# A mixer's layout split into two halves of the partitions, with its core in 64x64 tiles of TensorE

## The reference, cut to what matters

```python
# mixer: per channel d a linear recurrence with 64 states, B and C elementwise
def mixer(x, ...):                       # x is already layernorm(x) of the layer
    xn = layernorm(x) * ln_gamma + ln_beta
    dA = exp(-exp(log_A) * dt[:, None]); dB = B_param * dt[:, None]
    def step(h, u):
        h = dA * h + dB * u[..., None]
        y = einsum('dn,bdn->bd', C_param, h) + D_param * u
        return h, y
    ys = scan(step, 0, xn over time)
    return x + ys @ W_out.T + b_out
x = x + mixer(layernorm(x))
x = x + cross_attention(ctx, ctx, layernorm(x))
x = x + feed_forward(layernorm(x))       # w1, w2, h1, h2, w3
```

## Time and profile before

| | us |
|---|---|
| median of 3 runs | 1049.09 (1048.56 to 1052.2) |
| the profiled execution | 1048.15, its span 1046.4 |
| TensorE busy, whole span | 916.5 (88%) |
| VectorE, ScalarE, GpSimd busy | 576.4, 532.0, 206.2 |
| from 254.3 us on (feed-forward of all blocks, attention of 1 to 7) | 792.1, TensorE busy 773.1 |

### The profile page before, as it was taken

How to read it: one execution, slowest core, us unless ns; L and a number is a source line. 1 busy time by engine, 2 the same in 40 slices (tenths; PEclk the granted TensorE clock), 3 DMA queues, 4 the chain that set the end, 5 groups by cost and what they waited for, 6 DMA issues and landing times.

```text
span 1046.4 us, 15287 instructions
## 1 busy us (share of the span) xinstructions
PE 916.5 (88%) x5059; PEld 726.4 (69%) x5059; DVE 576.4 (55%) x948; ACT 532.0 (51%) x784; POOL 206.2 (20%) x239
## 2 busy tenths in 40 slices
PE   3200998976999999999999999999999999999996
PEld 0000988854778777877787778777877877787885
DVE  6598886663555555545454654555455555453421
ACT  2356675231665366446635663575366536645431
POOL 2365364100400130022003100400040014002000
PEclk9999999995999999999999999999999999999999
DMA  8984332134000200010001001100100020001000
GB/s 256 340 324 142 106 110 77 61 120 187 1 1 1 86 0 0 20 65 0 0 35 50 0 0 45 40 0 0 53 32 0 0 85 0 0 20 41 1 1 22
DMA packets 13502, 60.70 MB, mean 58 GB/s; under 512 B 2579, under 2 KB 4246, under 8 KB 12598
## 3 DMA queue, kind: packets, MB, share of 16 engines
q1 hardware_dynamic: 13382, 60.32, 16.8%
q10 hardware_dynamic: 64, 0.07, 0.0%
q0 software_dynamic: 32, 0.00, 0.0%
HBM read 46.09 MB, written 23.72 MB: 67 GB/s over the span
## 4 chain that ended last, share of the span: by engine, by line
PE 71%; DVE 12%; issue 9%; ACT 4%; DMA 2%; POOL 1%; DVEq 1%; POOLq 0%; ACTq 0%; SPq 0%
PE pair L1050 43%; PE pair L1037 9%; PE pair L1009 3%; PE pair L998 3%; PE pair L469 2%; PE pair L1025 2%; PE pair L461 2%; PE pair L509 2%; PE pair L975 1%; PE pair L1018 1%; DMA V<-V 1%; DVE V L348 1%; DMA ring<-kernel_rows 1%; DVE vbuf L898 1%; DVE V L347 1%
## 5 line engine op out<-in xcount | busy, mean ns | idle before, releaser
L751 ACT ACTIVATE vbuf<-pair,scl 128x512 f32<-128x512 f32 x128 | 87.8, 686 | 237.2 <-PE pair L1050 231.4
L1050 PE MATMUL pair<-h1hi,h_turned 128*128 128x512 f32 x512 | 204.1, 399 | 1.5 <-DVE h1lo L869 1.5
L1050 PE MATMUL pair<-h2hi,h_turned 128*128 128x512 f32 x512 | 202.6, 396 | 0.0
L1050 PE MATMUL pair<-h1lo,h_turned 128*128 128x512 f32 x512 | 199.8, 390 | 0.0
L1050 PE MATMUL pair<-h2lo,h_turned 128*128 128x512 f32 x512 | 199.6, 390 | 0.0
L869 DVE TENSOR_TENSOR h1lo<-vbuf,h1hi 128x512 fp32r<-128x512 f32 x80 | 57.7, 721 | 119.5 <-ACT h1hi L752 118.7
L1050 PEld LDWEIGHTS pair<-h1hi,h_turned 128*128 128x128 f32 x512 | 96.1, 188 | 34.5 <-issue 10.5
L1050 PEld LDWEIGHTS pair<-h2hi,h_turned 128*128 128x128 f32 x512 | 96.1, 188 | 25.2 <-issue 5.9
L869 DVE TENSOR_TENSOR h2lo<-vbuf,h2hi 128x512 fp32r<-128x512 f32 x64 | 44.2, 690 | 123.5 <-ACT h2hi L752 123.5
L1037 PE MATMUL pair<-zThi,w_turned 128*128 128x512 f32 x256 | 105.6, 413 | 5.3 <-DVE vbuf L898 2.7
L1050 PEld LDWEIGHTS pair<-h2lo,h_turned 128*128 128x128 f32 x512 | 96.2, 188 | 19.3
(11 more groups left out here) (117 smaller groups left out, 1484.0 us busy)
## 6 DMA issues: line engine op xcount, KB each, us to landing
h_turned<-d_h SPq DMA_DIRECT2D x2, 4096.0 KB, 14.3
xres<-in_x SPq DMA_DIRECT2D x8, 512.0 KB, 7.0
ring<-alpha_rows SPq DMA_DIRECT2D x16, 256.0 KB, 3.7
ring<-kernel_rows SPq DMA_DIRECT2D x16, 256.0 KB, 3.5
x_rows<-x1t SPq DMA_DIRECT2D x8, 512.0 KB, 2.6
xr<-x_rows SPq DMA_DIRECT2D x8, 512.0 KB, 3.5
out<-xr SPq DMA_DIRECT2D x8, 512.0 KB, 2.6
x_rows<-xres SPq DMA_DIRECT2D x7, 512.0 KB, 2.6
```

Of the source, the lines that this page charges most:

```text
L751: e.activation(vb[:, s % 2, :], h_ps[s % 4], ACT.Gelu, scale=sc)
L1050: ins = e.matmul(bank, w[:, k, m * P:(m + 1) * P], src[part][:, k, :], start=(k == 0 and part == 0), stop=(k == HC - 1 and part == 1))
```

## The change

The host hands over a second copy of x, `xs`, with channels 0 to 127 on partitions 0 to 63 and 128 to 255 on 64 to 127, the partition within a half being the step in a chunk. `tok` [128, 64 chunks, 128] holds it, is normed in place and takes y in the end. `GG` has the kernel entries, `EE` all state matrices (loaded at once in the front; `xres` lies on the same memory and is loaded group by group later), `TT` two buffers of Toeplitz matrices for 16 channels of each half. The statistics of a token lie in two halves of the partitions and are put together in small steps (`chain_step`) for 16 chunks at a time. The core has 16 iterations (`NOCT`) of 8 channels in each half, written out without loops, and three products for a channel, each on 64 rows and 64 columns; the carried product of an iteration runs in the next one, two channels late (`LAG`). The residual base is made in the core and after it. Waits of attention and projection are split between `k_in` (xW, keys, scl) and `w_in`. GpSimd and SP work as in the excerpts. The doublings and the steps of the tail are as they were, `y_turn` reads `tok[:, 8 * i + c, :]`.

```diff
+    def tt_load(e, g):
+        for h in range(2):
+            e.dma_start(TT[g % 2][L * h:L * h + L, :],
+                        bass.AP(t["kr_h"], (8 * h + g) * (GRP * L), [[1, L], [1, GRP * L]])).then_inc(T_in[g % 2], 16)
...
+        e.wait_ge(al_st, 32)
+        for g in range(NGRP):
+            for h in range(2):
+                e.dma_start(EE[L * h:L * h + L, GRP * g:GRP * g + GRP, :].rearrange("p d n -> p (d n)"),
+                            bass.AP(t["alS_h"], (8 * h + g) * (GRP * N), [[0, L], [1, GRP * N]])).then_inc(E_in[g], 16)
+        e.dma_start(bo[:, :], a["ab"].partition_broadcast(P)).then_inc(wo_in, 16)
...
+            tt_load(e, g)
+        for n in ("w1", "w2", "w3", "h1"):
+            e.dma_start(t["d" + n], a[n]).then_inc(w_d, 16)
+        for n in ("xW", "keys", "scl"):
+            e.dma_start(t[n], a[n]).then_inc(k_in, 16)
+        for g in range(NBLK):
+            e.wait_ge(h_ps, 2 * g + 2)
+            e.dma_start(xres[:, 4 * g:4 * g + 4, :], a["x"][:, 4 * g:4 * g + 4, :]).then_inc(xr_in[g], 16)
+            if g == 4:
+                e.wait_ge(w_d, 64)
+                for n in ("w1", "w2"):
+                    e.dma_start(t[n].bitcast(F32), t["d" + n]).then_inc(w_in, 16)
+        for n in ("h1", "w3"):
+            e.dma_start(t[n].bitcast(F32), t["d" + n]).then_inc(w_in, 16)
+        e.dma_start(t["dh2"], a["h2"]).then_inc(w_d, 16)
...
+        def inverse(b):
+            e.wait_ge(chain, 10 * b + 10)
+            here = slice(SB * b, SB * b + SB)
+            e.tensor_tensor(rs[:, :, here], sv[:, :, here], mhalf[:, :, :], ALU.pow).then_inc(powd, 1)
 
         def gamma(g):
+            e.wait_ge(z_rdy, 8 * g + 8)
+            v = tok[:, 8 * g:8 * g + 8, :]
+            e.tensor_tensor(v, v, gam[:, :].unsqueeze(1).to_broadcast([P, 8, P]), ALU.mult).then_inc(z_g, 1)
+        inverse(0)
+        e.wait_ge(bc_in, 64)
+        inverse(1)
+        gamma(0)
+        gamma(1)
+        inverse(2)
+        gamma(2)
+        gamma(3)
+        inverse(3)
+        gamma(4)
+        gamma(5)
+        for h in range(2):
+            rows = slice(L * h, L * h + L)
+            e.wait_ge(shift, 4)
+            e.wait_ge(z_g, 6)
+            e.tensor_scalar_add(rsn[rows, :], rs[rows, 0, h:BC:2], 1.0).then_inc(natural, 1)
+            e.wait_ge(natural, 2 * h + 1)
+            e.tensor_scalar_add(ngn[rows, :], ng[rows, 0, h:BC:2], 0.0).then_inc(natural, 1)
+
+        def mask(g):
+            e.wait_ge(T_in[g % 2], 32 * (g // 2 + 1))
+            e.wait_ge(natural, 4)
+            e.wait_ge(base_b, 4 * max(g - 4, 0))
+            for h in range(2):
+                e.wait_ge(t_mask, 2 * g + h)
+                v = TT[g % 2][L * h:L * h + L, :].rearrange("p (d t) -> p d t", d=GRP)
+                e.affine_select(out=v, in_=v, compare_op=ALU.is_ge, fill=0.0, base=L - 1,
+                                pattern=[[0, GRP], [-1, L]], channel_multiplier=-1).then_inc(t_mask, 1)
+
+        def bias(tile):
+            if tile == 0:
+                e.wait_ge(wo_in, 32)
+            e.wait_ge(base, tile + 1)
+            e.wait_ge(t_mask, min(2 * (tile // 4 + 5), 2 * NGRP))
+            e.tensor_tensor(xres[:, tile, :], xres[:, tile, :], bo[:, :], ALU.add).then_inc(base_b, 1)
+        for g in range(4):
+            mask(g)
+        for g in range(4, NGRP):
+            mask(g)
...
+        def row_evac(v):
+            for h in range(2):
+                u = 2 * v + h
+                e.wait_ge(k_ps, v + 1)
+                if u >= 4:
+                    e.wait_ge(kr_st[u % 4], 16)
+                e.activation(ksb[:, u % 4, :], kps[v % 2][h], ACT.Copy).then_inc(k_ev, 1)
+            for h in range(2):
+                u = 2 * v + h
+                e.wait_ge(k_ev, u + 1)
+                c = (1 - h) * (P * L) + v * 2048
+                e.dma_start(kr[0, c:c + 2048].rearrange("(q m) -> q m", q=4), ksb[0:P:32, u % 4, :]).then_inc(kr_st[u % 4], 16)
+
+        def norm_apply(b):
+            e.wait_ge(shift, b + 1)
+            for c in range(SB * b, SB * b + SB):
+                e.activation(tok[:, c, :], tok[:, c, :], ACT.Identity, bias=ng[:, 1, c:c + 1], scale=rs[:, 1, c:c + 1]).then_inc(z_rdy, 1)
+
...
+        def entry_exp(g):
+            e.wait_ge(E_in[g], 32)
+            v = EE[:, GRP * g:GRP * g + GRP, :].rearrange("p d n -> p (d n)")
+            e.activation(v, v, ACT.Exp, scale=esc[:, :]).then_inc(e_rdy, 1)
 
         def residual_base(g):
+            e.wait_ge(xr_in[g], 16)
+            for j in range(4 * g, 4 * g + 4):
+                e.activation(xres[:, j, :], xres[:, j, :], ACT.Identity, bias=ngn[:, j:j + 1], scale=rsn[:, j:j + 1]).then_inc(base, 1)
+        for v in range(4):
+            row_evac(v)
+        e.wait_ge(const, 9)
+        norm_apply(0)
+        entry_exp(0)
+        norm_apply(1)
+        entry_exp(1)
+        entry_exp(2)
+        norm_apply(2)
+        entry_exp(3)
+        norm_apply(3)
+        for g in range(4, NGRP):
+            entry_exp(g)
+        e.wait_ge(natural, 4)
+        for o in range(NOCT):
+            e.wait_ge(y_ps, o + 1)
+            e.activation(tok[:, :, OCT * o:OCT * o + OCT], yps[o % 4].rearrange("p (i c) -> p c i", i=OCT), ACT.Copy).then_inc(y_out, 1)
+            if o % 2 == 1 and o // 2 + 2 < NGRP:
+                tt_load(e, o // 2 + 2)
+            if o % 2 == 1 and o >= 5:
+                residual_base((o - 5) // 2)
+        residual_base(NBLK - 2)
+        residual_base(NBLK - 1)
 
...
+        def stats(b, steps):
+            for c in range(SB):
+                if c % 8 == 0:
+                    e.wait_ge(x_in[2 * b + c // 8], 16)
+                e.bn_stats(st4[:, b % 2, c, 0:2, :].rearrange("p a m -> p (a m)"), tok[:, SB * b + c, :]).then_inc(stat, 1)
+                if steps and c >= 4:
+                    steps.pop(0)()
+
+        def beta(g):
+            e.wait_ge(*((z_g, g + 1) if g < 6 else (z_h, g - 5)))
+            v = tok[:, 8 * g:8 * g + 8, :]
+            e.tensor_tensor(v, v, bet[:, :].unsqueeze(1).to_broadcast([P, 8, P]), ALU.add).then_inc(z_b, 1)
+        stats(0, [])
+        stats(1, [lambda n=n: chain_step(0, n) for n in range(11)])
+        stats(2, [lambda n=n: chain_step(1, n) for n in range(11)])
+        e.wait_ge(bc_in, 64)
+        beta(0)
+        beta(1)
+        stats(3, [lambda n=n: chain_step(2, n) for n in range(11)])
+        e.wait_ge(k_ps, 4)
+        for row in (0, N):
+            e.tensor_copy(GG[row:row + 1, :, L - 1], edit[row:row + 1, 1, :]).then_inc(g_row, 1)
+        for n in range(10):
+            chain_step(3, n)
+        beta(2)
+        beta(3)
+        chain_step(3, 10)
+        for k in range(2):
+            e.memset(dec[:, k, :].rearrange("p (b c) -> p b c", c=CH)[:, :, 0], 0.0).then_inc(dec0, 1)
+        beta(4)
+        beta(5)
...
+        def state(o, c):
+            i = OCT * o + c
+            for h in range(2):
+                rhs = tok5[L * h:L * h + L, i, :, 0:CH - 1]
+                rows = slice(N * (1 - h), N * (2 - h))
+                out = hps[o % 2][rows, c * BC:(c + 1) * BC].rearrange("p (b c) -> p b c", b=BATCH)[:, :, 1:CH]
+                ins = e.matmul(out, EE[L * h:L * h + L, i, :], rhs, start=True, stop=True)
+            return ins
+
+        def within(o, c):
+            i = OCT * o + c
+            for h in range(2):
+                rows = slice(L * h, L * h + L)
+                ins = e.matmul(yps[o % 4][rows, c * BC:(c + 1) * BC], TT[o // 2 % 2][rows, (i % GRP) * L:(i % GRP + 1) * L], tok[rows, :, i], start=(c == 0), stop=False)
+            return ins
+
+        def carried(o, c):
+            i = OCT * o + c
+            for h in range(2):
+                rows, other = slice(L * h, L * h + L), slice(N * (1 - h), N * (2 - h))
+                ins = e.matmul(yps[o % 4][rows, c * BC:(c + 1) * BC], GG[other, i, :], scan[other, o % 2, c * BC:(c + 1) * BC], start=False, stop=(c == OCT - 1))
+            return ins
+        e.wait_ge(z_b, 8)
+        e.wait_ge(h_zero, 2)
         e.wait_ge(e_rdy, 1)
-        states(0, 0, (h_scan, 1))
-        turn(0, False)
-        with e.Fori(1, DM // OCT // 4 - 1) as it:
-            turn(it, False)
-        turn(DM // OCT // 4 - 1, True)
-
+        for c in range(OCT):
+            ins = state(0, c)
+        ins.then_inc(h_ps, 1)
+        for o in range(NOCT + 1):
+            if o < NOCT and o % 2 == 0:
+                e.wait_ge(t_mask, o + 2)
+            if o + 1 < NOCT and o % 2 == 1:
+                e.wait_ge(e_rdy, o // 2 + 2)
+            if o >= 1:
+                e.wait_ge(h_scan, o)
+            if o == 1:
+                e.wait_ge(g_row, 9)
+            if 4 <= o < NOCT:
+                e.wait_ge(y_out, o - 3)
+            for c in range(OCT + LAG):
+                if c < OCT and o + 1 < NOCT:
+                    ins = state(o + 1, c)
+                    if c == OCT - 1:
+                        ins.then_inc(h_ps, 1)
+                if c < OCT and o < NOCT:
+                    ins = within(o, c)
```

(69 more changed lines are left out.)

414 lines of the change are left out of this document (163 added, 251 removed).

## The result

The changed kernel takes 1058.38 us (median of 5 runs, 1056.89 to 1062.09) against 1049.09: a ratio of 1.0093 with a 95% interval from 1.0065 to 1.012. It is slower by 0.9%, 9.3 us; I had forecast 1047.3. The profiled execution has a span of 1059.1 us, 12.7 more than before.

What follows compares the result with a forecast made beforehand. Bounds: a VectorE-GpSimd-ScalarE relay (front), a load-mask-product chain (core), TensorE turns and projections (tail). Terms -2.8 + 2.7 - 1.6 = -1.7 us gave 1047.3 against 1049.09; own range 1040 to 1053, eight in ten 1033 to 1062.

Steps and rivals of the forecast that it cites:

- Front: Stage before the core: shorter relay of VectorE, GpSimd and ScalarE, powers 5.6 us each; core starts at 83.5 instead of 102.6.
- Quadrants: Core products on TensorE: quadrants overlap fully, an iteration takes 1.9 us warm and 3.6 at the slow pace.
- the first rival: Earlier front (power 1.67 us) or iterations of 1.9 instead of 3.6 us: near 1035, chance 0.25.
- Iterations 0 to 2: First iterations of the core, before the load-bound cycles: 8.3 us.
- The cycle: Core, two iterations: 7.6 us from y's evacuation through load and masks, plus 3.6 for the iteration: 11.2, six times 67.2.
- 0.3 for the 512 KB of x: Core, each cycle: what the x load that SP issues just ahead adds to the Toeplitz load, 0.3 us.
- Plus 1 where 2 MB of w1 and w2 share the queues: Core, one cycle: these weights add 1 us to one Toeplitz load.
- vblk: Tail: vblk lands 28.8 us after the last state products, behind queued loads; turn_q(0) 32.6 after them, at 191.7.
- 1.1 more for a slow clock and cheaper turns: Tail: slow TensorE products after idling cost 2.7 us, turns 4 to 7 give back 1.6.
- later loads: Rival: front at 92, or Toeplitz loads sharing queues more, 1.5 us more a cycle: 1058, chance 0.15.
- Quadrants in a row: Rival, core: quadrants run one after the other, an iteration 5.6 us, 14 to 17 us more: 1062, chance 0.15.
- A clock that stays up: Part of the first rival, core: iterations of 1.9 instead of 3.6 us give 10 us; near 1035, shared chance 0.25.

Runs made afterwards that it cites:

- the first run with them: Changed kernel plus 56 TensorE products that nobody reads ahead of each mask wait from the third group on: 1058.32 us.
- the run with 48: Changed kernel with each x load held until the next Toeplitz group landed, plus 48 unread products ahead of mask waits from the fourth group: 1051.1 us.
- the power split: Changed kernel with GpSimd's front power on 16 elements, not 32, the other half behind the first two masks: 1055.23 us; on top of the other edits 1005.06.
- the other edits: Changed kernel with Toeplitz groups loaded earlier, vblk ahead of h1, w3 and h2, w1 and w2 behind vblk, residual norms earlier: 1009.15 us.

## Why the prediction was wrong

The chain of each stage was right; the step that failed is the size of two terms of the core's cycle, what x and what w1 and w2 add to a load, and with it the sign. The profiled execution lies 14.4 us above the sum (1060.8 against 1046.4), the median 11.1 above 1047.3. By the steps of the sum:

**Front: right.** The core starts at 85.1 (83.5 forecast). A power of 32 elements took 5.43 to 5.47 us (5.6), once 6.3 beside VectorE's adds; statistics 0.20 each; GpSimd's multiplication by gamma 2.32 (2.4), two in 4.64; the row stores ended at 32 instead of 36.5. The step from two small sizes to 32 elements was the one I doubted most, and it held. That the total is so near is in part luck. Three of VectorE's four steps behind a power (L381) took 2.3 us each while GpSimd multiplied by gamma, where I had 0.16 for a small step (the first, alone, took 0.19), and the last power ended at 72.6 instead of 69.7; what followed took 12.5 us instead of 13.8. Error +1.6.

**Quadrants: right in kind.** I took an iteration as 32 x 0.058 = 1.9 us, and 3.6 slow. They run side by side, but at the fast clock an iteration takes 2.6 us, 0.027 a record; from the first product behind a mask to y it takes 3.5 to 3.7 at the slow one. The 3.6 was read from the pace of the earlier trace rows alone: the view of the kernel before gives a granted clock of 1.00 from 103 to 106, so that the clock was the reason there is not shown. It fits what the changed kernel took at 0.50. The clock's price, which I took as 1.7 us an iteration in the first rival, is about 1. Since the second iteration of a pair is faster than 3.6, TensorE idles some 6 us in a gap (5.64 ahead of 102.83, 6.16 ahead of 114.99) and not 4. Iterations 0 to 2 took 9.5 instead of 8.3: error +1.2.

**The cycle: right in kind, mis-sized.** From the evacuation of y to the next product 7.9 to 8.7 us went by, not 7.6, and where it was worst 14.0; the iteration that delivers y took the 3.6 forecast. The term "0.3 for the 512 KB of x" is one that failed: the load took 4.9 to 5.8 instead of 4.2 + 0.3, because x, issued just ahead, was in the queues. Without it, it took 4.0 to 4.3. The five common cycles took 59.9 instead of 56.0: error +3.9, and +0.2 to the last state products. "Plus 1 where 2 MB of w1 and w2 share the queues" failed by more: that load took 11.03 and its cycle 17.7 instead of 12.2, error +5.5; with w1 and w2 elsewhere the load took 5.99 and the cycle 12.7. I had rows for the size: 4 MB land in some 10 us of their own, and what is issued behind them lands behind them, so that 2 MB in front are about 5 us and x's 512 KB above 1. I used that for `vblk` and not for TT. In those rows both transfers stand on SyncE's queue; here ScalarE issues the load and SyncE x, w1 and w2, and the load was held up all the same (11.03, and 10.07 where SyncE issued it too).

**vblk: right.** 30.8 us after the last state products, 28.8 forecast; turn_q(0) came 34.2 after them instead of 32.6: error +1.6. That `vblk`, and not the norms or TensorE, sets it, is shown by two runs that move one each. Behind turn_q(0) the way to the first gated product took 61.6 us against 59.8 before, where I had 1.1 more for a slow clock and cheaper turns: +0.7, and the feed-forward part gave back 0.5.

These make 1.6 + 1.2 + 3.9 + 0.2 + 5.5 + 1.6 + 0.7 - 0.5 = 14.2, nearly all of one sign. The two large ones, 9.4 together, were loads that meet other loads; I had put both at their lower end and left "later loads" to a rival of 0.15 at 1058. That the time came out there is luck in the number: by its own terms, 6 x 1.5 = 9 on 1047.3, that rival gives 1056.3, and the core's loads missed by 0.8 in five cycles and 5.5 in one, the rest coming from the front and the tail. Each microsecond that a load loses in the core is paid six times over, since the cycle is the bound; a term with a factor of six needed its upper end in the forecast.

**The rivals.** "Quadrants in a row" is refuted (1098.6 when they are). "A clock that stays up" was not the case: it was 0.50 behind all six masks (103 to 105, 116 to 118, 127 to 129, 144 to 148, 156 to 158, 168.5 to 170.5). "Later loads" was the case, by the mechanism of x and w1 and w2 in front, not by stores under copies.

## What to carry to other kernels

When a change makes the arithmetic of a stage much shorter, work out the chain of buffer, load, mask and first use anew, and ask from which event the load is issued: it has to be the last reader of the buffer, here the within products, and not a later step that happens to be on the same engine. Then list what else is issued in the microseconds before that load, by any engine, with its size; in a double-buffered loop whose cycle is bound by a load, each of them is paid once a cycle. And what is small and needed soon (`vblk`, 128 KB) goes ahead of what is large and needed late (9 MB of weights) on its queue.

## What the runs showed that I had not expected

**TensorE busy, and its clock still down.** With products on one quadrant at a time the granted clock was 0.50 for the whole core although TensorE had no gap (1126 records in 100 us, above); in the changed kernel, where the interleaved products begin at 85.1, it was 0.57 from 87 to 89 and 1.00 from 89 to 91. One quadrant at a time does not always bring it down: the 56 unread products of the first run with them took 6 us at 1.00 in the second gap (113.55), and those of the run with 48 at 0.50 in one gap and at 1.00 in the other four. Only this is shown; which feature of the work makes the difference is not.

**A shift that costs 4 us in untouched code.** With the power split, the part from the first gated product on took 795.9 us instead of 791.7 on top of the other edits, and 796.2 instead of 791.6 alone. In each block of the feed-forward part some of VectorE's subtractions into h1lo took longer, and TensorE waited for them 14 times instead of 7 (4.2 us instead of 1.6), its weight loads 14 times instead of 8 (10.2 instead of 4.7). Instructions on the tile h1lo, VectorE, 100 us of the feed-forward part, the changed kernel and the one with the power split:

```profile
L887 DVE TENSOR_TENSOR h1lo<-vbuf,h1hi x10: 683/691/1047, 389.7 to 461.8; 128x512 fp32r<-128x512 f32 x10
```

```profile
L895 DVE TENSOR_TENSOR h1lo<-vbuf,h1hi x10: 684/692/1224, 381.7 to 454.4; 128x512 fp32r<-128x512 f32 x10
```

The same instruction with the same shapes has the same median and a longest of 1.22 instead of 1.05 us. From one block to the next the same subtractions lie 99.6 us apart in the changed kernel and 100.3 in the other; seven blocks at that difference, 0.66 us each, make the 4 to 5 us. GpSimd's bias adds (x1t<-x1t,xbo) took 855 ns in the mean instead of 977 over the whole part, so the two engines meet at other moments than before; that this is the cause is my reading and was not tested.
